# Attention with a row-wise maximum in the score matmul: the first 512 queries take their maxima by one more matmul, no early burst of maxima, and the weights lead both load queues

## The chip, the cores and the metric

The kernel runs on one core of one Trainium2 chip. The metric is the device time of one execution in microseconds (us). Three runs of the kernel before gave 602.68, 604.81 and 605.72 us; the median is 604.81 us.

Engines are called as the profile calls them: PE is TensorE's matmul, PEld its weight load, DVE is VectorE, ACT is ScalarE, POOL is GpSimd, SP is SyncE. SPq and ACTq are the sequencers of SP and ACT issuing transfers.

## The reference

One attention layer and one mixture-of-experts layer, each followed by a residual and a layer norm. The input is x of 2048 tokens by 128 channels, float32. Cut to what matters here:

```
k_eff = W_dq.T @ W_uq.T @ W_uk          # weights alone, folded per head
v_eff = W_uv.T @ W_o.T
c_kv  = x @ W_dkv.T
q_lat = (x @ W_dq.T @ W_uq.T) . k_eff    # 16 heads of 8 channels
attn  = softmax(causal(q_lat . c_kv / sqrt(8)))
y     = (attn . c_kv) . v_eff
x     = layernorm(x + y)
x     = layernorm(x + moe(x))            # 8 experts, top 2, capacity 80, two groups of 1024 tokens
```

The softmax of a row of scores needs that row's maximum, since the scores are large.

## The kernel before

**The parts ahead of attention.** SP issues the six weight transfers, ACT issues the four transfers of x (256 KB each) and the router's. PE first waits for all six weights (`s_w`), turns or multiplies them (L970 to L972), then turns the first block of x (`turn_x(0)`, L979), and alternates with DVE until the folded weights `qw`, `kw`, `vw` exist. From these it makes keys, queries (L999) and values (L1003) of each 512 tokens. Keys and queries are each split by ACT and DVE into three bf16 parts (L595 to L738), which SP stores to DRAM and loads again, laid out by head, into `kT` and `qT` (L437, L448), in transfers of 384 KB, or 96 KB for the first block's four head groups. Partitions 0 to 125 carry the products of parts; partitions 126 and 127 of `kT` hold ones, so that whatever stands in partitions 126 and 127 of `qT` is added to every score of that query.

**Attention.** The 2048 queries are four supers of 512; 16 heads are four groups of four. A unit is one super with one group of heads, so there are 16 units, units 0 to 3 being the first 512 queries. A unit of super s has 4(s+1) steps, one for each 128 keys, and 160 steps in all: `STEPS`, with `FIRST[u]` the first step of unit u (0, 4, 8, 12, 16, 24, ...). One step is, for each of four heads, one matmul `scT` of 128 keys by up to 512 queries (L1041), on a diagonal tile one more matmul of 128 columns that masks (L1045), an exponential on ACT (L629), and two steps later (`LAG`) the product with the values into `acc` (L1058, 8 matmuls). For the four steps of the first super the widths are 512, 384, 256 and 128 queries. `scT` is a ring of three banks (`SRING`).

**The maxima.** Before unit u can start, each of its rows needs its maximum. It is found from a second set of scores, `sc`, with the queries on partitions: for each item one matmul (L1020) of 128 to 512 columns and one DVE instruction (L749 for a full block, L754 for a diagonal one, which adds the mask) into `part_max`. `sc` is a ring of three banks too. Items of a unit of super 0 have 128, 256, 384 or 512 columns, four of each. `max_rows(u)` joins the partial maxima on DVE and splits the negative maximum in two bf16 halves, `turn_max(u)` turns them on PE (L1027) to 8 rows by 512 queries, `keep_maxT(u)` copies them on ACT to `maxT[u % 2]` (L610), and `max_to_rows(u)` issues a transfer from `maxT` into partitions 126 and 127 of `qT` (L615). PE waits for it before the unit's first score:

```python
if j == 0 and h == 0:
    pe.wait_ge(max_in[u % 2], 16 * (u // 2 + 1))
```

**The order.** Unit 0's 16 items are done ahead of the steps. Then `EARLY` = 16 items, those of unit 1, are issued in one burst before step 0, behind `turn_max(0)`. All further items are woven into the steps by `woven()`, between the four heads of a step. It fills from the last step backwards: an item of w columns counts w + 60, a step takes up to 2400, or `RUSH_WORK` = 3000 in the first `RUSH` = 20 steps, and no item of unit u may stand behind `max_step(u)` = `FIRST[u]` - `LEAD` - 1. `LEAD` is 5. `schedule()` puts `max_rows(u)` into step `max_step(u)` and the `max_turn` that calls `turn_max` and `keep_maxT` at the end of the step after it. Each engine runs its own program in this order; semaphores tie them.

**Behind the first super** (`FIRST[GROUPS]` on) come the normalisation and the experts, which run beside later attention steps. SP issues the experts' weights (2 MB each, L483 and L484) as soon as the splits are stored and loaded.

Of the kernel before, what the change touches and what calls it, by code (L numbers as in the profile page):

```python
# [26 lines left out]
P = 128  # L27
# [3 lines left out]
QUERIES = 512  # L31
SUPERS = T // QUERIES
TILES = T // P
QT = QUERIES // P
HG = 4
GROUPS = HEADS // HG
UNITS = SUPERS * GROUPS
# [6 lines left out]
PRING = 12  # L44
SRING = 3
AHEAD = 1
EARLY = 16
LEAD = 5
ITEM_WORK = 2400
RUSH, RUSH_WORK = 20, 3000  # L50
LAG = 2
BIG = -1e38

# [15 lines left out]
F32, BF16, U32 = mybir.dt.float32, mybir.dt.bfloat16, mybir.dt.uint32  # L69
ALU = mybir.AluOpType  # L70
# [5 lines left out]
def super_of(u):  # L76
    return u // GROUPS
# [7 lines left out]
FIRST = [sum(unit_steps(v) for v in range(u)) for u in range(UNITS + 1)]  # L85
# [8 lines left out]
def is_diagonal(u, j):  # L94
    return j >= QT * super_of(u)
# [11 lines left out]

def max_step(u):

    return max(0, FIRST[u] - LEAD - 1)  # L110


def item_work(i):
# [112 lines left out]
def program(nc, x_d, wdq_d, wuq_d, wdkv_d, wuk_d, wuv_d, wo_d, router_d, wi_d, wo2_d, out_d):  # L226
    ctx = ExitStack()
    with ctx:
        def sb(name, shape, dt=F32):
            return ctx.enter_context(nc.sbuf_tensor(name, shape, dt))  # L230

        def sem(name):
            return ctx.enter_context(nc.semaphore(name))
# [10 lines left out]
        x = sb("x", [P, TILES, C])  # L244
# [33 lines left out]
        wdq, wuq, wdkv, wuk = early(0, LAT, C), early(1, C, LAT), early(2, LAT, C), early(3, C, LAT)  # L278
        wuv, wo, wuqT, woT = early(4, C, LAT), early(5, C, C), early(6, LAT, C), early(7, C, C)
# [4 lines left out]
        ident16 = sb("ident16", [P, P], BF16)  # L284
# [11 lines left out]
        maxT = [sb(f"maxT{i}", [2 * HG, QUERIES], BF16) for i in range(2)]  # L296
# [26 lines left out]
        slot_out = sb("slot_out", [P, 2 * MT], U32)  # L323
        einT = sb("einT", [P, SLOTS])
        x1T = einT[:, 0:QUERIES]
        hT = [sb(f"hT{i}", [P, FC, CAP]) for i in range(2)]

        back2 = sb("back2", [P, MT, C])
# [2 lines left out]
        scT = [ctx.enter_context(nc.psum_tensor(f"scT{i}", [P, QUERIES], F32)) for i in range(SRING)]  # L331
# [5 lines left out]
        s_w = sem("s_w")  # L337
        s_router = sem("s_router")
        s_x = [sem(f"s_x{i}") for i in range(SUPERS)]
        s_ffw = sem("s_ffw")  # L340
        s_const = sem("s_const")
        s_const_v = sem("s_const_v")
        s_rows = sem("s_rows")
        q_rows = sem("q_rows")
        q_rows0 = sem("q_rows0")
# [17 lines left out]
        maxT_kept = sem("maxT_kept")  # L363
        max_in = [sem(f"max_in{i}") for i in range(2)]
        scT_made = sem("scT_made")
# [48 lines left out]
        def token_rows(d, a, b):  # L414
            return d[a * P:b * P, :].rearrange("(n p) c -> p n c", p=P)
# [2 lines left out]

        @block.sync
        def _(sp):  # L420
            for dst, src in ((wuq, wuq_d), (wuk, wuk_d), (wo, wo_d), (wdq, wdq_d), (wuv, wuv_d), (wdkv, wdkv_d)):
                sp.dma_start(dst, src).then_inc(s_w, 16)

            def clear_slots():
                sp.wait_ge(s_const, 3)
# [51 lines left out]
            for b in range(LAST + 1):  # L477
# [7 lines left out]
                for name, arg in TASKS[b]:  # L485
                    if name == "max_turn" and arg in (GROUPS + 1, 2 * GROUPS + 1):
                        s = super_of(arg) + 1
# [11 lines left out]
                    if name == "norm_out" and arg[0] == "moe":  # L499
                        k = arg[1]  # L500
# [6 lines left out]
        def _(pool):  # L507
# [12 lines left out]
            nc.gpsimd.affine_select(out=later16[:, :], in_=later16[:, :], compare_op=ALU.is_ge, fill=BIG, base=0,  # L520
                                    pattern=[[1, P]], channel_multiplier=-1).then_inc(s_const, 1)

            tri = causal[:, QUERIES - P:QUERIES]
            nc.gpsimd.affine_select(out=tri, in_=tri, compare_op=ALU.is_ge, fill=BIG, base=0,
                                    pattern=[[-1, P]], channel_multiplier=1).then_inc(s_const, 1)
# [42 lines left out]
            for b in range(LAST + 1):  # L568
                for name, arg in TASKS[b]:
                    if name == "slots" and arg < MOE_GROUPS - 1:  # L570
                        scatter(arg)
                    if name == "norm_ln" and arg[0] == "attn" and arg[1] < SUPERS - 1:
                        k = arg[1]
# [8 lines left out]

        @block.scalar
        def _(act):
            for i in range(SUPERS):
                act.dma_start(x[:, i * QT:(i + 1) * QT, :], token_rows(x_d, i * QT, (i + 1) * QT)).then_inc(s_x[i], 16)
            act.dma_start(router[:, :], router_d).then_inc(s_router, 16)
            nc.scalar.preload_act_table_set("natural_log_exp_and_others")
# [15 lines left out]

            def keep_maxT(u, bank):

                if u >= 2:

                    act.wait_ge(max_in[u % 2], 16 * (u // 2))
                nc.scalar.activation(maxT[u % 2][:, :], bank.bitcast(BF16)[0:2 * HG, 0:QUERIES], ACT.Copy).then_inc(maxT_kept, 1)  # L610

            def max_to_rows(u):
                act.wait_ge(maxT_kept, u + 1)
                g = u % GROUPS
                act.dma_start(qT[super_of(u) % 2][MROW:MROW + 2, g * HG:(g + 1) * HG, :], maxT[u % 2][:, :]).then_inc(max_in[u % 2], 16)  # L615
# [350 lines left out]
        def _(pe):  # L966
# [64 lines left out]
            def scores(b, h):  # L1031

                u, j = STEPS[b]
                s, off = super_of(u), first_query(u, j)
                if j == 0 and h == 0:
                    pe.wait_ge(max_in[u % 2], 16 * (u // 2 + 1))
                n = HG * b + h
                if n >= SRING:
                    pe.wait_ge(exp_done, n - SRING + 1)
                head = u % GROUPS * HG + h  # L1040
                ins = nc.tensor.matmul(scT[n % SRING][:, 0:QUERIES - off], kT[:, head, j * P:(j + 1) * P],  # L1041
                                       qT[s % 2][:, head, off:QUERIES], start=True, stop=True, skip_group_check=True)
                if is_diagonal(u, j):

                    ins = nc.tensor.matmul(scT[n % SRING][:, 0:P], ident16[:, :], later16[:, :], start=False, stop=True,  # L1045
                                           skip_group_check=True)
                ins.then_inc(scT_made, 1)
# [27 lines left out]
                scores_for_max(i)  # L1075
            pe.wait_ge(v_kept, SUPERS)
            pe.wait_ge(s_const_v, 2)
            pe.wait_ge(maxT_kept, AHEAD)

            def task(name, arg):  # L1080
# [107 lines left out]
```

## Time and profile before

| quantity | value |
|---|---|
| median of three runs | 604.81 us (602.68 to 605.72) |
| the profiled execution's own time | 605.5 us |
| its span | 603.8 us |
| mean granted TensorE clock | 0.958 |
| busy: PE, DVE, ACT, POOL | 87%, 74%, 58%, 10% |
| attention step 0 begins (first score matmul issued) | about 50.2 us |
| step 19 begins | about 110.8 us |

The span is from the first to the last instruction that the profile shows; the execution's time holds 1.7 us more. Busy shares are means over stages with different limits, so this text reads stretches of time. The time of a step's beginning is that of the first L1020 or L1041 matmul behind the step before it.

### The profile page before, as it was taken

The numbers are of one execution on the slowest core, as the hardware profiler recorded it, in microseconds if no ns is written. First come the engines' busy times: TensorE is split into PE (matmuls) and PEld (weight loads), VectorE is DVE, ScalarE is ACT, GpSimd is POOL, SyncE is SP. The second block draws the span as 40 slices with busy tenths as digits, with TensorE's granted clock in tenths as the row PEclk, the third lists the DMA queues.
The fourth block names the chain that finished last, engine by engine and source line by source line (L and its number), as shares of the span: only waits on it lengthen the run. The fifth ranks groups of instructions, "written<-read, shape, count | busy, mean of one in ns | idle before, by whom it ended". The sixth has DMA issues, their size and how long they took to land.

```text
span 603.8 us, 10349 instructions
## 1 busy us (share of the span) xinstructions
PE 523.9 (87%) x3445; PEld 220.7 (37%) x3491; DVE 447.2 (74%) x1311; ACT 349.5 (58%) x751; POOL 63.1 (10%) x64
## 2 busy tenths in 40 slices
PE   4966999889999989879989999899999988946990
PEld 2523333333333333234445333233333221223890
DVE  4786999798987988957657888879889814347616
ACT  0614556656767765755655777577777779820230
POOL 9400000000000000640000540000000000000040
PEclk9967999999999999999999999999999999985996
DMA  3489992200000300110000250000000000000024
GB/s 85 126 213 209 202 279 61 45 2 2 2 2 1 80 2 2 40 54 1 2 11 1 48 37 1 1 2 1 1 2 1 2 1 19 19 0 1 8 37 49
DMA packets 25410, 24.90 MB, mean 41 GB/s; under 512 B 2314, under 2 KB 22668, under 8 KB 25356
## 3 DMA queue, kind: packets, MB, share of 16 engines
q1 hardware_dynamic: 21660, 20.42, 13.9%
q0 software_dynamic: 1280, 2.62, 3.7%
q10 hardware_dynamic: 2416, 1.18, 0.7%
q8 instruction: 28, 0.46, 0.3%
q14 instruction: 26, 0.21, 0.1%
HBM read 16.81 MB, written 7.28 MB: 40 GB/s over the span
## 4 chain that ended last, share of the span: by engine, by line
PE 52%; issue 22%; DVE 13%; ACT 5%; DMA 3%; POOL 3%; ACTq 1%; SPq 0%; DVEq 0%; POOLq 0%
PE acc L1058 15%; PE sc L1020 13%; PE scT L1041 11%; DVE unused L754 3%; ACT probs L629 3%; POOL exp_in L551 2%; DVE part_max L749 2%; PE scT L1045 2%; PE ms L1143 2%; PE ms L1149 2%; DMA qT<-maxT 1%; DVE kT L909 1%; PE ms L1092 1%; ACT maxT L610 1%; DVE stats L783 1%
## 5 line engine op out<-in xcount | busy, mean ns | idle before, releaser
L629 ACT ACTIVATE probs<-scT 128x512 f32<-128x512 f32 (+3 forms) x640 | 302.6, 539 | 131.3 <-PE scT L1045 77.4
L749 DVE TENSOR_REDUCE part_max<-sc 128x1 f32<-128x512 f32 x384 | 249.9, 684 | 26.9 <-PE sc L1020 23.7
L1020 PE MATMUL sc<-kT,qT 126*128 126x512 bf16 (+3 forms) x640 | 223.2, 360 | 16.1 <-DVE part_max L749 7.6
L1041 PE MATMUL scT<-qT,kT 128*128 128x512 bf16 (+3 forms) x594 | 201.8, 349 | 10.1 <-ACT probs L629 8.6
L1058 PE MATMUL acc<-probs,v 128*9 128x512 f32 (+3 forms) x1280 | 146.5, 531 | 0.4
L754 DVE CUSTOM_DVE_ANT_0 unused<-sc,causal 128x128 bf16<-128x128 f32 (+3 forms) x256 | 120.2, 484 | 32.9 <-PE sc L1020 31.4
L1020 PEld LDWEIGHTS sc<-kT,qT 126*128 126x128 bf16 x640 | 62.4, 99 | 145.9 <-DVE part_max L749 82.9
L1041 PEld LDWEIGHTS scT<-qT,kT 128*128 128x128 bf16 x640 | 62.2, 99 | 70.6 <-ACT probs L629 39.9
L1045 PE MATMUL scT<-later,ident 128*128 128x128 bf16 x256 | 55.9, 221 | 4.9 <-DMA qT<-maxT 4.3
L1058 PEld LDWEIGHTS acc<-probs,v 128*9 128x9 f32 x1280 | 19.2, 88 | 47.3 <-ACT probs L629 33.2
L1045 PEld LDWEIGHTS scT<-later,ident 128*128 128x128 bf16 x256 | 25.6, 100 | 19.3 <-issue 0.7
L575 POOL TENSOR_TENSOR res<-res,x 128x512 f32<-128x512 f32 x3 | 3.8, 1269 | 227.3 <-DVEq L802 227.3
L810 DVE TENSOR_TENSOR nt<-rs 128x2 f32<-128x2 f32 (+1 forms) x12 | 1.9, 160 | 29.7 <-ACT rs L651 29.7
L754 DVE DVE_READ_ACCUMULATOR2_ANT part_max<- 128x1 f32 x256 | 21.2, 83 | 0.0
L565 POOL DMA_INDIRECT back<-exp_out,slot_out x16 | 15.3, 954 | 53.4 <-DMA exp_out<-x 48.9
L610 ACT ACTIVATE maxT<-ms 8x512 bf16<-8x512 bf16 x16 | 9.4, 586 | 16.1 <-PE ms L1027 16.1
L649 ACT ACTIVATE lnv<-var 128x4 f32<-128x4 f32 x12 | 2.6, 218 | 27.7 <-DVE var L938 27.7
L551 POOL DMA_INDIRECT exp_in<-x,slot_in x16 | 15.7, 980 | 24.8 <-DVE slot_in L877 20.2
L578 POOL IOTA kT<- 128x640 f32 x1 | 0.7, 665 | 147.6 <-PE scT L1045 147.6
L565 POOL DMA_INDIRECT x<-exp_out,slot_out x8 | 7.6, 956 | 72.9 <-DMA exp_out<-x 70.8
L794 DVE RECIPROCAL recip<-ms 128x16 f32<-128x16 f32 x13 | 3.3, 257 | 14.7 <-PE ms L1092 14.7
L531 POOL MEMSET kT<- 64x4096 uint32 x4 | 13.9, 3506 | 0.1
(182 smaller groups left out, 340.2 us busy)
## 6 DMA issues: line engine op xcount, KB each, us to landing
kT<-parts_k SPq DMA_DIRECT2D x9, 384.0 KB
qT<-parts_q SPq DMA_DIRECT2D x9, 384.0 KB
wi<-in_L_ffn_wi SPq DMA_DIRECT2D x1, 2048.0 KB, 18.1
parts_k<-wi SPq DMA_DIRECT2D x3, 384.0 KB, 4.1
parts_q<-wi SPq DMA_DIRECT2D x3, 384.0 KB, 5.0
kT<-parts_k SPq DMA_DIRECT2D x12, 96.0 KB
qT<-parts_q SPq DMA_DIRECT2D x12, 96.0 KB
x<-in_L_attn_x ACTq DMA_DIRECT2D x4, 256.0 KB, 4.3
```

What stands on the lines that cost most here:

```text
L531: nc.gpsimd.memset(rows, one_pair).then_inc(s_rows, 1)
L551: pool.indirect_dma_start(exp_in_d[:, :], bass.IndirectOffsetOnAxis(slot_in[:, n:n + 1], 0), x1[:, g * MT + n % MT, :], None).then_inc(sca ...
L565: pool.indirect_dma_start(dst, None, exp_out_d[g][:, :], bass.IndirectOffsetOnAxis(slot_out[:, n:n + 1], 0)).then_inc(gathered[PIECES * g ...
L610: nc.scalar.activation(maxT[u % 2][:, :], bank.bitcast(BF16)[0:2 * HG, 0:QUERIES], ACT.Copy).then_inc(maxT_kept, 1)
L629: nc.scalar.activation(probs[n % PRING][:, 0:width], scT[n % SRING][:, 0:width], ACT.Exp).then_inc(exp_done, 1)
L749: nc.vector.tensor_reduce(dst, sc[i % SRING][:, :], AX.X, ALU.max).then_inc(sc_used, 1)
L754: nc.vector.tensor_tensor_reduce(unused[i % 2][:, 0:w], sc[i % SRING][:, 0:w], causal[:, QUERIES - w:QUERIES], 1.0, 3 * BIG, ALU.add, ALU. ...
L1020: nc.tensor.matmul(sc[i % SRING][:, 0:w], qT[s % 2][0:MROW, head, qt * P:(qt + 1) * P], kT[0:MROW, head, c * QUERIES:c * QUERIES + w], sta ...
L1041: ins = nc.tensor.matmul(scT[n % SRING][:, 0:QUERIES - off], kT[:, head, j * P:(j + 1) * P], qT[s % 2][:, head, off:QUERIES], start=True, ...
L1045: ins = nc.tensor.matmul(scT[n % SRING][:, 0:P], ident16[:, :], later16[:, :], start=False, stop=True, skip_group_check=True)
L1058: ins = nc.tensor.matmul(acc[32 * h:32 * h + VC, off:QUERIES], v[:, j, head, :], probs[(HG * b + h) % PRING][:, 0:QUERIES - off], start=(j ...
L1143: ins = nc.tensor.matmul(bank[:, f * CAP:(f + 1) * CAP], wi[:, e, f * P:(f + 1) * P], einT[:, e * CAP:(e + 1) * CAP], start=True, stop=True)
```

## The change

It does six things. (1) For units 0 to 3 the maxima no longer go by a transfer to `qT`: after each score matmul a second one adds them into the same bank, with `maxT` (8 rows by the step's queries) as the moving side and a constant `pick16` as the stationary side, which picks rows h and h + 4 for head h; PE waits for ACT's copy instead of the transfer. From unit 4 on nothing changes there. (2) `EARLY` becomes 0: unit 1's items are woven into steps 0 and 1. (3) `LEAD` becomes `LEADS`: 2 for units 0 to 3, 3 for unit 4, 5 for the others. (4) `RUSH_WORK` becomes 3300. (5) The weights are issued three on SP and three on ACT, and behind them x blocks 0 and 2 on SP, 1 and 3 on ACT. (6) POOL makes `pick16` with one more instruction, before it fills the rows of ones.

```diff
-EARLY = 16
-LEAD = 5
+EARLY = 0
+LEADS = [2] * GROUPS + [3] + [5] * (UNITS - GROUPS - 1)
 ITEM_WORK = 2400
-RUSH, RUSH_WORK = 20, 3000
+RUSH, RUSH_WORK = 20, 3300
...
-    return max(0, FIRST[u] - LEAD - 1)
+    return max(0, FIRST[u] - LEADS[u] - 1)
+
+
+def rows_sent(u):
+
+    return max(0, len(range(u % 2, u + 1, 2)) - len(range(u % 2, GROUPS, 2)))
...
+        pick16 = einT[0:2 * HG, 0:HG * P // 2].bitcast(BF16).rearrange("p (h k) -> p h k", h=HG)
...
         def _(sp):
-            for dst, src in ((wuq, wuq_d), (wuk, wuk_d), (wo, wo_d), (wdq, wdq_d), (wuv, wuv_d), (wdkv, wdkv_d)):
+            for dst, src in ((wuq, wuq_d), (wdq, wdq_d), (wdkv, wdkv_d)):
                 sp.dma_start(dst, src).then_inc(s_w, 16)
+            for i in range(0, SUPERS, 2):
+                sp.dma_start(x[:, i * QT:(i + 1) * QT, :], token_rows(x_d, i * QT, (i + 1) * QT)).then_inc(s_x[i], 16)
...
+            nc.gpsimd.tensor_tensor(pick16[:, :, :], ident16[0:2 * HG, 0:HG].unsqueeze(2).to_broadcast([2 * HG, HG, P]),
+                                    ident16[0:2 * HG, HG:2 * HG].unsqueeze(2).to_broadcast([2 * HG, HG, P]), ALU.add).then_inc(picked, 1)
...
         def _(act):
-            for i in range(SUPERS):
+            for dst, src in ((wo, wo_d), (wuk, wuk_d), (wuv, wuv_d)):
+                act.dma_start(dst, src).then_inc(s_w, 16)
+            for i in range(1, SUPERS, 2):
                 act.dma_start(x[:, i * QT:(i + 1) * QT, :], token_rows(x_d, i * QT, (i + 1) * QT)).then_inc(s_x[i], 16)
...
             def keep_maxT(u, bank):
-                if u >= 2:
-
-                    act.wait_ge(max_in[u % 2], 16 * (u // 2))
+                if 2 <= u < GROUPS + 2:
+
+                    act.wait_ge(scT_made, HG * FIRST[u - 1])
+                elif u >= 2:
+
+                    act.wait_ge(max_in[u % 2], 16 * rows_sent(u - 2))
...
             def max_to_rows(u):
+                if super_of(u) == 0:
+                    return
...
                 if j == 0 and h == 0:
-                    pe.wait_ge(max_in[u % 2], 16 * (u // 2 + 1))
+                    if s:
+                        pe.wait_ge(max_in[u % 2], 16 * rows_sent(u))
+                    else:
+                        pe.wait_ge(maxT_kept, u + 1)
...
+                if s == 0:
+
+                    nc.tensor.matmul(scT[n % SRING][:, 0:QUERIES - off], pick16[:, h, :], maxT[u % 2][:, off:QUERIES],
+                                     start=False, stop=True, skip_group_check=True)
...
             pe.wait_ge(s_const_v, 2)
+            pe.wait_ge(picked, 1)
```

Worked out from the two versions of `woven()`, the items of each stretch of steps are these; from step 19 on both orders are the same:

| steps | items, columns before | items, columns after |
|---|---|---|
| ahead of step 0 (unit 1) | 16, 5120 | 0 |
| 0 to 3 | 24, 6656 | 26, 7424 (10, 6, 0, 10 in the four steps) |
| 4 to 7 | 25, 9728 | 30, 10496 |
| 8 to 11 | 22, 9600 | 24, 10752 |
| 12 to 15 | 22, 9344 | 27, 10752 |
| 16 to 18 | 18, 6912 | 20, 7936 |

## Rows read from the trace of the kernel before

**Rows 1.** The page: busy shares, and the span in 40 equal slices.

```profile
PE 523.9 (87%) x3445; PEld 220.7 (37%) x3491; DVE 447.2 (74%) x1311; ACT 349.5 (58%) x751; POOL 63.1 (10%) x64
...
PE   4966999889999989879989999899999988946990
```

**Rows 2.** The chain that ended last, in order of time: start us, us, what.

```profile
3.45 4.26 DMA wo<-in_L_attn_W_dkv
...
40.49 0.60 ACT maxT L610
41.10 9.00 DMA qT<-maxT
```

**Rows 3.** Windows: us, busy (instructions) of each engine, granted clock, DMA share, GB/s.

```profile
40.70:47.50 6.80, 5.42 (x15) 1.34 (x13) 6.77 (x32) 0.38 (x1) 0.00 (x0) 0.50 0.83 147
47.50:50.60 3.10, 0.00 (x0) 0.14 (x2) 0.03 (x2) 0.00 (x0) 0.00 (x0) 0.50 0.84 157
50.60:63.00 12.40, 11.45 (x80) 5.77 (x80) 9.95 (x54) 7.08 (x17) 0.00 (x0) 0.85 0.98 255
63.00:76.50 13.50, 12.26 (x94) 5.01 (x95) 12.51 (x44) 7.53 (x18) 0.00 (x0) 1.00 0.92 182
76.50:89.50 13.00, 11.88 (x90) 4.85 (x90) 12.17 (x37) 7.44 (x18) 0.00 (x0) 1.00 1.04 290
89.50:101.70 12.20, 11.63 (x88) 4.67 (x88) 11.26 (x33) 7.49 (x18) 0.00 (x0) 1.00 0.16 52
101.70:112.00 10.30, 9.91 (x59) 3.01 (x61) 10.04 (x33) 7.67 (x15) 0.00 (x0) 1.00 0.59 118
```

**Rows 4.** Timeline of the first 21 us: start, us, engine, line, what, idle before.

```profile
0.81 2.14 ACTq L586 DMA_DIRECT2D x<-in_L_attn_x  x4
...
2.30 3.47 DVE L705 MEMSET qT<- 64x4096 uint32 x1 [0.91 <-issue]
...
7.84 0.39 PE L970 MATMUL sc<-ident,wo 128*64 128x128 f32 x1 [7.84 <-DMA wo<-in_L_attn_W_dkv]
...
8.78 1.12 PE L979 MATMUL scT<-ident,x 128*128 128x128 f32 x4
...
20.39 0.60 PE L979 MATMUL scT<-ident,x 128*128 128x128 f32 x4
```

**Rows 5.** DMA issues of the first weights and of x, us to landing.

```profile
wo<-in_L_attn_W_uq SPq DMA_DIRECT2D x1, 32.0 KB, 2.4
...
DMA to landing us min/median/max: 3.3/4.3/4.9
```

**Rows 6.** Timeline of PE in unit 3: scores, masks, and the value products.

```profile
90.18 0.38 PE L1041 MATMUL scT<-qT,kT 128*128 128x512 bf16 x1
90.40 0.22 PE L1045 MATMUL scT<-later,ident 128*128 128x128 bf16 x1
...
97.67 1.05 PE L1058 MATMUL acc<-probs,v 128*9 128x512 f32 x8
...
98.87 0.22 PE L1041 MATMUL scT<-qT,kT 128*128 128x128 bf16 x1
98.93 0.22 PE L1045 MATMUL scT<-later,ident 128*128 128x128 bf16 x1
```

**Rows 7.** Timeline of DVE in items of 128 and of 512 columns.

```profile
40.71 0.29 DVE L754 CUSTOM_DVE_ANT_0 unused<-sc,causal 128x128 bf16<-128x128 f32 x1 [0.99 <-PE sc L1020]
40.92 0.08 DVE L754 DVE_READ_ACCUMULATOR2_ANT part_max<- 128x1 f32 x1
40.92 0.29 DVE L754 CUSTOM_DVE_ANT_0 unused<-sc,causal 128x128 bf16<-128x128 f32 x1
...
100.89 0.68 DVE L754 CUSTOM_DVE_ANT_0 unused<-sc,causal 128x512 bf16<-128x512 f32 x1
101.50 0.08 DVE L754 DVE_READ_ACCUMULATOR2_ANT part_max<- 128x1 f32 x1
```

**Rows 8.** Timeline of ACT: unit 4's copy and its transfer.

```profile
89.61 0.59 ACT L610 ACTIVATE maxT<-ms 8x512 bf16<-8x512 bf16 x1 [0.69 <-PE ms L1027]
90.23 0.64 ACTq L615 DMA_DIRECT2D qT<-maxT  x1
```

**Rows 9.** Windows around the end of the bulk transfers.

```profile
92.00:94.00 2.00, 2.00 (x20) 0.93 (x18) 1.88 (x6) 1.89 (x5) 0.00 (x0) 1.00 0.14 41
```

**Rows 10.** POOL's nearest elementwise instruction: duration min, median, max in ns.

```profile
L575 POOL TENSOR_TENSOR res<-res,x x3: 1262/1267/1277, 127.5 to 382.2; 128x512 f32<-128x512 f32 x3
```

More of the change, by code:

```diff
@@ L342, in program @@
         s_const_v = sem("s_const_v")
+        picked = sem("picked")
         s_rows = sem("s_rows")
```

## The prediction, made before the changed kernel ran

> **What bounds the kernel now.** I read the page first: PE is busy 87% of the span and DVE 74%, and the first slices show PE at 4, 9, 6 and 6 tenths [rows 1]. These are means; the change touches only the stretch up to step 18, because both orders are the same from step 19 on. So I read that stretch alone. The chain of waits shows two transfers that end last there. One is a weight, issued at 3.45 us and landing 4.26 us later. The other is unit 0's row of maxima, 9.00 us from 41.10 to 50.10 [rows 2]. The windows then say what was done in those 9 us: the early burst keeps DVE busy 6.77 us, then DVE has 0.03 us of work in 3.10 us, and PE none [rows 3]. From 50.6 us on, DVE is busy 9.95 of 12.4, then 12.51 of 13.5, 12.17 of 13.0, 11.26 of 12.2 and 10.04 of 10.3 us [rows 3]. PE's busy shares are as high, but they count each matmul's tail: a 128-column matmul counts 0.22 us while the next starts 0.06 us after it [rows 6]. By starts, a 512-column matmul takes 0.22 us and a 128-column one 0.055 us. DVE, not PE, sets the pace of the woven steps: an item costs it 0.21 us at 128 columns and 0.61 us at 512 [rows 7], that is 0.08 us plus 0.133 per 128 columns, while PE needs 0.055 per 128.
>
> I measure the stretch from ACT's copy of unit 0's maxima (ready at 41.1 us) to the start of step 19 (110.8 us): 69.7 us.
>
> **The load end, edits 5 and 6.** PE's first instruction waits 7.84 us for the last weight; x is there before it, since the first turning of x at 8.78 follows with no wait [rows 4]. ACT issues all four x transfers from 0.81 to 2.95 us, so SP's late weights run beside 1 MB of x. Afterwards each queue issues three weights at about 0.5 us each, the last at about 1.9 us. The first weight took 2.4 us to land and an x block at least 3.3 us [rows 5]. So the weights are there at about 4.4 and x block 0, issued at about 2.4, at about 5.8 us. PE's three weight products (0.94 us, 7.84 to 8.78) are done by then, and DVE's memset of `qT` ends at 5.77 [rows 4], just in time. The first turning starts at 5.8 instead of 8.78: 3.0 us earlier. With the median 4.3 us to landing and an issue as late as 2.8, it is 7.1 and 1.7 us. The same shift should pass down the chain of PE and DVE to 41.1 us, as each link is released by the one before it. One thing may not shift: the turning of four x tiles counts 1.12 us at 8.78 and 0.60 at 20.39 [rows 4], though the granted clock reads 1.00 in both places, so PE speeds up somewhere before 20.4 us. If that moment stays fixed in time, about half of a microsecond per microsecond of shift is lost. I take 2.6 us, bounds 1.2 and 3.3. POOL's extra instruction on 8 partitions is bounded by 0 and the 1.27 us of a 128x512 one [rows 10]. It delays the first memset of ones, which ended near 7 us and is first needed by a load at 24.6 us; I take nothing. If that cover went, it would cost its 1.27 us.
>
> **The row transfer and the burst, edits 1 and 2.** The 9.0 us wait of unit 0 goes. What it covered does not: the burst's 16 items cost DVE 16 x 0.08 + 40 x 0.133 = 6.6 us (6.77 in the window [rows 3]) and are now woven in. Only DVE's idle time can be won: the 3.1 us ahead of step 0 plus about 0.4 us until the first new item, and whatever later idle goes.
>
> The Trainium skill, page "DMA: Bandwidth & Descriptors", section "Anatomy of one DMA — SWDGE (gpsimd) path", gives a transfer a fixed 2.0 us. The trace does not agree for this one: 9.0 us for 8 KB, at a DMA share of 0.83 [rows 2, 3]. By the page's figure the burst would already hide the wait, nothing would be won at step 0, and the sum below would be about 603.5; the measured 9.0 us is what I use.
>
> **The picks, edit 1.** Sixteen steps of four heads get one matmul more: 64 of them, 4 x 4 x (512 + 384 + 256 + 128) = 20480 columns. No row shows a matmul with an 8-row moving side. The nearest is the mask matmul, accumulating into the same bank straight behind the score matmul with no gap [rows 6]. At 0.055 us per 128 columns the picks take PE 8.8 us, 2.2 us a unit. The lower bound is nothing on the path, where PE waits for DVE anyway; the upper is all 8.8 us. The weight loads run beside the matmuls as the others do.
>
> **The new order, edits 2 to 4.** After the change a unit of steps 4 to 15 costs PE: scores and picks 10240 columns 4.4, masks 0.9, values about 2.6 (0.97 for a 512-wide step by starts, less for the narrower) [rows 6], items about 4.6, turning 0.2: 12.7 us. DVE has 10496, 10752 and 10752 columns: 13.3, 13.1 and 13.3 us, plus about 0.5 us of `max_rows`, so 13.8, 13.6, 13.8. DVE still leads over a unit, but in each unit's widest step PE needs about 3.6 us against DVE's 3.4, so taking the larger in each step gives 14.1, 13.8 and 14.1. Steps 16 to 18 are 9.85 + 0.5, so 10.4. Steps 0 to 3 have 7424 columns, 9.8 + 0.5 on DVE; but step 0 has 4608 score, pick and mask columns and 2304 item columns, and the granted clock is at 0.5 (1.2 GHz) when it starts. After the restart at 50.6 us it averaged 0.85 over 12.4 us [rows 3], which is 3.7 us at half; the same here makes 4440 columns in 3.7 us and the other 2472 in 1.0, so 4.7 us on PE against 3.2 on DVE, and step 2 has no items, which leaves DVE about 0.9 us idle. I take 13.0. The sum is 13.0 + 14.1 + 13.8 + 14.1 + 10.4 = 65.4 us. The same sum for steps 4 to 18 before is 12.6 + 12.2 + 12.0 + 9.1 = 45.9 against 47.8 measured (63.0 to 110.8), 1.9 us of small waits through the three-bank rings. With PE at some 90% instead of 75% these grow: I take 2.5 us. That makes 67.9 us against 69.7: a gain of 1.8 us.
>
> The bounds: the stretch's DVE work is 62.7 us (sum of the seven windows' DVE time [rows 3]); with 0.4 us to start, 63.1 is the floor, a gain of 6.6. If the picks lie wholly on the path, the stretch is 69.7 − 9.4 (start of step 0) + 6.8 (burst items) + 8.8 = 75.9, a loss of 6.2, which the work sums make unlikely; half on the path is 71.5, a loss of 1.8.
>
> The shorter leads cost nothing for units 1 to 3: PE reaches the turning one step, some 3 us, after DVE's last item, and ACT's copy takes 0.6 us [rows 8] within the following step. ACT's copy of unit 2 waits for the scores of unit 0, long done. For unit 4 the transfer stays. Its turning ends step 13; 1.5 us later it is issued, and two steps (about 6.5 us) after the turning PE wants it: 5.0 us to land. It is issued at about 89 us, when the bulk is ending (before, the share is 0.14 by 92 [rows 9], and the load end moves it earlier). I cost it at nothing; bounds 0 and 4.0, if it takes 9.0 us as unit 0's did.
>
> **The sum.** 2.6 + 1.8 = 4.4 us. The profiled execution took 605.5 us (span 603.8 and 1.7 around it) and would take 601.1. It stood 0.7 above the median of 604.81, so the prediction is 600.4 us.
>
> **The rivals.**
> - *The picks hide wholly behind DVE.* For it: DVE leads every unit's sum. Against: PE would have almost no slack in the wide steps. The stretch is near its floor: 6.6 + 2.6 = 9.2 us, 595.6.
> - *PE becomes the bound (the slower side).* The place is steps 0 to 15, the price 8.8 us of picks. It decides once more than about 60% of them lie on the path: the 2.6 us of the load end and 9.4 − 6.8 = 2.6 of the wait are then used up. At 90% the time is 604.8 − 2.6 − 2.6 + 7.9 = 607.5. For it: PE's busy share already reads above 0.9 [rows 3], and ring waits make a coupled pair slower than either. Against: the spacing by starts.
> - *The load end gives nothing*, because the same 1.2 MB still lands by about 7.5 us: 604.8 − 1.8 = 603.0. The Trainium skill speaks for this one: "DMA: Bandwidth & Descriptors", section "Issuing engines are not separate DMA queues", says that issuing from two engines saves only sequencer time. No row shows what the weights would do ahead of x.
> - *Unit 4's row comes late* by up to 4.0 us at step 16, in place of unit 0's: 604.4.
>
> **How the numbers follow.** Forecast 0.46, spread 598.5 to 602.5; picks hidden 0.14; PE the bound 0.15; load end empty 0.14; unit 4 late 0.11. Three us, 0.5%, is about what a measurement can tell from no change. Faster by more than that: most of the forecast (0.42) and the hidden picks (0.14), 0.56. Same: the empty load end, unit 4 late, the forecast's rest, 0.31. Slower: 0.13. The range of 596 to 605 leaves out most of the PE-bound case and the end of the hidden one.
>
> **What would show it.** Right: the first turning of x near 5.8 us, unit 0's copy on ACT ready near 38.5, the first score matmul within 0.5 us of it, step 19 at about 106.4; DVE busy 61 to 63 us in between with 5 to 6 us idle; no PE wait on a transfer at step 16. Wrong: a first turning after 7.5 us; DVE waiting for PE's `sc` by more than 8 us; a PE wait on `qT<-maxT` near 100 us; or a granted clock of 0.5 that outlasts step 0.

## The result, and the profile after

The changed kernel took 617.74 us (median of four runs, 616.52 to 618.49) against 604.75 for the kernel before: a ratio of 1.022, 95% interval 1.020 to 1.024. It is 13.0 us slower. 600.4 us with a range of 596 to 605 was forecast. Two runs, both of front_only below (609.6 and 1724.5 us), were disturbed and count in no ratio.

The page of the changed kernel, busy shares and the new group, the pick matmul, which is L1068 here (the columns are busy time, mean ns, idle time before):

```profile
PE 544.2 (88%) x3509; PEld 224.8 (36%) x3555; DVE 449.5 (73%) x1311; ACT 351.6 (57%) x751; POOL 64.1 (10%) x65
...
L1068 PE MATMUL scT<-maxT,einT 8*128 8x512 bf16 (+3 forms) x64 | 21.6, 337 | 0.8 <-issue 0.4
```

PE is busy 20.3 us more than before, DVE 2.3 [rows 1]. The added PE time is not the 8.8 us of columns that the prediction counted.

Timeline of the changed kernel's first 8 us and of ACT's copy of unit 0's maxima:

```profile
4.73 0.39 PE L990 MATMUL sc<-ident,wo 128*64 128x128 f32 x1 [4.73 <-DMA wo<-in_L_attn_W_dkv]
...
6.85 1.12 PE L999 MATMUL scT<-ident,x 128*128 128x128 f32 x4 [1.10 <-DMA x<-in_L_attn_x]
...
18.64 0.95 PE L999 MATMUL scT<-ident,x 128*128 128x128 f32 x4
...
39.10 0.59 ACT L628 ACTIVATE maxT<-ms 8x512 bf16<-8x512 bf16 x1 [9.15 <-PE ms L1047]
```

The weights lead: PE begins 3.1 us earlier than in [rows 4], waits 1.1 us for x, and turns it 1.9 us earlier. The copy comes 1.4 us earlier [rows 2]. So the load end works, by 1.4 us. Everything after it is worse. Windows of the changed kernel, cut at about the first score of units 1, 2, 3 and 4; the first begins just ahead of ACT's copy:

```profile
38.50:62.60 24.10, 22.75 (x97) 7.49 (x98) 11.30 (x55) 8.16 (x18) 0.00 (x0) 0.55 0.89 219
62.60:79.60 17.00, 16.71 (x117) 6.17 (x114) 14.42 (x59) 8.06 (x18) 0.00 (x0) 1.00 1.00 207
79.60:96.20 16.60, 16.45 (x112) 5.99 (x110) 14.02 (x39) 8.06 (x18) 0.00 (x0) 1.00 0.51 161
96.20:113.20 17.00, 16.52 (x111) 6.06 (x111) 14.04 (x43) 7.85 (x18) 0.00 (x0) 1.00 0.01 2
```

DVE is busy for 14.0 to 14.4 of some 17 us a unit, where it had 12.51 of 13.5 [rows 3]: it waits for PE, and PE is the bound. The view of waits in 38 to 124 us (engine, line, what it waited for: us in total, times, longest) says so too:

```profile
DVE unused L774 <- PE sc L1040: 17.6, 22, 4.9
```

The first window has a second trouble. Its mean granted clock is 0.55, though PE is busy 22.75 of 24.10 us. Finer windows of the changed kernel show when it rose:

```profile
56.00:60.00 4.00, 4.00 (x25) 1.62 (x25) 1.20 (x9) 1.25 (x3) 0.00 (x0) 0.50 0.94 319
60.00:62.00 2.00, 1.99 (x16) 0.95 (x18) 1.80 (x11) 0.59 (x3) 0.00 (x0) 0.93 0.84 236
```

PE ran at 0.5, that is 1.2 GHz, until just after 60 us, through some 20 us in which it was busy all the time. The spacing inside a head shows the other part. PE and its weight loads (PEld) in unit 2 of the changed kernel, at full clock:

```profile
80.92 0.38 PE L1064 MATMUL scT<-qT,kT 128*128 128x512 bf16 x1
81.23 0.38 PE L1068 MATMUL scT<-maxT,einT 8*128 8x512 bf16 x1
81.55 0.23 PE L1072 MATMUL scT<-later,ident 128*128 128x128 bf16 x1
81.61 0.49 PE L1040 MATMUL sc<-kT,qT 126*128 126x256 bf16 x2
...
81.23 0.09 PEld L1068 LDWEIGHTS scT<-maxT,einT 8*128 8x128 bf16 x1 [0.43 <-issue]
81.54 0.10 PEld L1072 LDWEIGHTS scT<-later,ident 128*128 128x128 bf16 x1 [0.23 <-issue]
```

A 512-column score is followed by the next matmul after 0.22 us in [rows 6], and here after 0.31. The pick is followed by the mask after 0.32. The pick's weight load does not start until the score's columns are through (81.23), nor the mask's load until the pick's are (81.54). Each change, from 128 rows to 8 and back, shows a load of 0.09 to 0.10 us. That is 0.2 us a pick on top of its 0.22 us of columns.

### The profile page after: what moved, and what is told of

Read it like the earlier page. It is cut to its first block, busy times and chain, and to the rows that moved or that the text cites. A ratio compares the mean times of both kernels' runs of the same rounds, so it can differ in the third digit from the quotient of the medians.

```text
span 616.5 us, 10474 instructions
## 1 busy us (share of the span) xinstructions
PE 544.2 (88%) x3509; PEld 224.8 (36%) x3555; DVE 449.5 (73%) x1311; ACT 351.6 (57%) x751; POOL 64.1 (10%) x65
## 4 chain that ended last, share of the span: by engine, by line
PE 57%; issue 20%; DVE 11%; ACT 5%; POOL 3%; DMA 2%; ACTq 1%; SPq 0%; DVEq 0%; POOLq 0%
PE acc L1085 15%; PE sc L1040 14%; PE scT L1064 12%; PE scT L1072 3%; PE scT L1068 3%; ACT probs L649 2%; POOL exp_in L564 2%; DVE unused L774 2%; DVE part_max L769 2%; PE ms L1171 1%; PE ms L1177 1%; DVE kT L929 1%; ACTq L635 1%; PE ms L1120 1%; ACT maxT L628 1%
## 5 line engine op out<-in xcount | busy, mean ns | idle before, releaser
L1040 PE MATMUL sc<-kT,qT 126*128 126x512 bf16 (+3 forms) x640 | 219.8, 359 | 14.4 <-DVE part_max L769 6.4
L774 DVE CUSTOM_DVE_ANT_0 unused<-sc,causal 128x128 bf16<-128x128 f32 (+3 forms) x256 | 121.2, 485 | 42.2 <-PE sc L1040 40.5
L1068 PE MATMUL scT<-maxT,einT 8*128 8x512 bf16 (+3 forms) x64 | 21.6, 337 | 0.8 <-issue 0.4
L578 POOL DMA_INDIRECT back<-exp_out,slot_out x16 | 15.2, 953 | 53.5 <-DMA exp_out<-x 48.9
L628 ACT ACTIVATE maxT<-ms 8x512 bf16<-8x512 bf16 x16 | 9.4, 586 | 17.6 <-PE ms L1047 17.5
```

What stands on the lines that cost most here:

```text
L578: pool.indirect_dma_start(dst, None, exp_out_d[g][:, :], bass.IndirectOffsetOnAxis(slot_out[:, n:n + 1], 0)).then_inc(gathered[PIECES * g ...
L774: nc.vector.tensor_tensor_reduce(unused[i % 2][:, 0:w], sc[i % SRING][:, 0:w], causal[:, QUERIES - w:QUERIES], 1.0, 3 * BIG, ALU.add, ALU. ...
L1040: nc.tensor.matmul(sc[i % SRING][:, 0:w], qT[s % 2][0:MROW, head, qt * P:(qt + 1) * P], kT[0:MROW, head, c * QUERIES:c * QUERIES + w], sta ...
L1068: nc.tensor.matmul(scT[n % SRING][:, 0:QUERIES - off], pick16[:, h, :], maxT[u % 2][:, off:QUERIES], start=False, stop=True, skip_group_ch ...
```

## The experiments

Line numbers differ a little between the kernels; the tiles' names tell which matmul is meant. All times stand against runs of the kernel before on the same chip.

### The picks on 128 rows, the order alone, the picks alone, the loads alone

**pad128** keeps all six edits, but widens the pick with rows of zeros:

```diff
-        maxT = [sb(f"maxT{i}", [2 * HG, QUERIES], BF16) for i in range(2)]
+        maxT = [sb(f"maxT{i}", [P, QUERIES], BF16) for i in range(2)]
-        pick16 = einT[0:2 * HG, 0:HG * P // 2]...
+        pick16 = einT[:, 0:HG * P // 2]...
```

(and a memset of `maxT` on POOL). Expected:

> The changed kernel, but with maxT and pick16 on all 128 partitions (rows 8 to 127 zero), so that the pick is a 128-row matmul with the same columns. Theory A (the switch): an 8-row matmul between 128-row ones keeps its own weight load and the next one's from running beside a matmul, about 0.1 us each, so 64 picks cost some 13 us beyond their columns; here the spacing from score to pick and from pick to mask falls from 0.31 and 0.32 us to about 0.22 and 0.22 at 512 columns, and the time from 617.7 to about 604 us. Theory B (the order): the time was lost by the missing burst and the shorter leads, whatever the picks' shape; the spacing may fall, but the time stays above 614 us. Theory C (the columns alone): the picks cost by their columns, and nothing changes by more than 1 us.

Measured: 603.98 us against 604.63, ratio 0.999 (0.998 to 1.000), 13.8 us under the changed kernel. Timeline of PE in its unit 3:

```profile
83.32 0.38 PE L1069 MATMUL scT<-qT,kT 128*128 128x512 bf16 x1
83.54 0.38 PE L1073 MATMUL scT<-maxT,einT 128*128 128x512 bf16 x1
83.76 0.22 PE L1077 MATMUL scT<-later,ident 128*128 128x128 bf16 x1
83.81 0.38 PE L1045 MATMUL sc<-kT,qT 126*128 126x512 bf16 x1
```

0.22, 0.22 and 0.05 us: the same columns with no load showing. The pick's load now starts 0.01 us after the score instead of behind it (PEld of pad128):

```profile
83.33 0.10 PEld L1073 LDWEIGHTS scT<-maxT,einT 128*128 128x128 bf16 x1
83.54 0.10 PEld L1077 LDWEIGHTS scT<-later,ident 128*128 128x128 bf16 x1
```

And the clock rose in the first step instead of after 20 us (windows of pad128):

```profile
40.00:42.00 2.00, 1.89 (x9) 1.10 (x10) 0.93 (x7) 0.53 (x1) 0.00 (x0) 0.50 0.84 150
42.00:44.00 2.00, 2.00 (x11) 1.01 (x10) 1.39 (x9) 0.94 (x3) 0.00 (x0) 0.74 0.87 123
```

Theory A's number is met, in part by luck: it put all 13 us down to the loads and had no term for the clock, to which some 5 of them belong (pad64 below). Theories B and C fall as explanations of the 13 us.

**order_only** is the kernel before with `EARLY = 0`, `LEADS` and `RUSH_WORK = 3300`. Expected:

> The kernel before with edits 2 to 4 alone (no burst, the shorter leads, 3300 per step); the rows still go by transfer, the loads as before. Theory A: the order costs little of the 13 us; step 0 still waits for the 9 us transfer, now with nothing under it, and unit 1's row may be late as well, so 604.8 plus 3 to 9 us: 608 to 614, and no part of it is PE's own work. Theory B: PE and DVE are out of step through units 0 to 3 even beside those waits, DVE idle on PE over 15 us in steps 0 to 15: 615 or more.

Measured: 615.70 us, ratio 1.019 (1.016 to 1.023). That is above theory A's 608 to 614 and at the lower edge of theory B's number, and DVE's 17.5 us of waiting for PE are over the 15 that theory B asked for. But half of them lie under a row transfer, so they are not waits beside it. The view of waits in 36 to 110 us, the two that matter:

```profile
DVE unused L754 <- PE sc L1020: 17.5, 11, 8.7
PEld scT L1041 <- DMA qT<-maxT: 13.2, 3, 8.5
```

Three times PE waits for a row transfer, the longest 8.5 us at step 0. DVE's longest wait for PE, 8.7 us, is under that one. So the new order is costly where rows still go by transfer: it needs the picks. This run does not tell what it costs beside them, and which share of the other 8.8 us of DVE's waiting belongs to the two later transfers stays open.

**picks_only** is the changed kernel with edits 2 to 5 undone. Expected:

> The changed kernel with edits 2 to 5 undone: burst of 16 items, lead 5, 3000 per step, loads as before; only the 8-row picks in place of the row transfers of units 0 to 3, and POOL's constant. Theory A: the picks alone cost more than the whole change did, since the load end's gain is missing: 64 x 0.4 = 26 us of PE time, less what DVE's pace hides (about 3 us a unit) and less the 3 us wait that goes: 604.8 + 10 to 16, so 615 to 621. Theory B: 604.8 + 8.8 of columns at most, less 3: under 610.

Measured: 619.76 us, ratio 1.025 (1.023 to 1.027), inside theory A's range. The picks alone, with the burst and the old leads, lose more than the whole change. Four of its five runs took 619.4 to 621.0 at a mean granted clock of 0.950; the profiled one took 612.9 at 0.959. In its trace the clock had risen to 1.00 by about the first pick (45.93 us), and stayed there (windows of picks_only):

```profile
44.00:48.00 4.00, 4.00 (x16) 1.15 (x15) 3.20 (x14) 1.22 (x3) 0.00 (x0) 0.80 0.85 140
48.00:52.00 4.00, 4.00 (x24) 1.60 (x23) 3.41 (x20) 2.64 (x5) 0.00 (x0) 1.00 0.94 191
```

So 8-row picks did not bring a risen clock down. Mean clocks of 0.950 and 0.959 over some 615 us are, by estimate, about 12 us more at 0.5, and the same program then took about 7 us more: the nearest thing here to a price of the clock by itself.

**front_only** is the kernel before with edit 5 alone. Expected:

> The kernel before with edit 5 alone: weights three on each queue, x behind them on both. All theories: the first turning of x at 6.85 us as in the changed kernel, unit 0's copy on ACT 1.4 us earlier, and the time 604.8 - 1.4 = 603.4 us (602.5 to 604). If unit 0's row transfer, which ends the wait at step 0, is bound by the bulk transfers around it and not by when it is issued, it is 604.5 or more.

Measured: 603.23 us, ratio 0.996 (0.994 to 0.998). The median is the 1.4 us that were expected. The interval allows 1 to 4 us, and the profiled run, which took 599.23 us, does not show the expected steps (timeline of ACT in front_only):

```profile
37.93 0.59 ACT L614 ACTIVATE maxT<-ms 8x512 bf16<-8x512 bf16 x1 [9.14 <-PE ms L1031]
45.24 3.44 ACT L633 ACTIVATE probs<-scT 128x512 f32<-128x512 f32 x6 [6.72 <-PE scT L1049]
```

Its copy stands 2.6 us earlier than before, not 1.4, and its row transfer took 5.83 us from 38.55, not 9.00. So the load end gives something, but this run does not pin it to 1.4 us, and the 9.0 us of the wait are no constant either: in order_only the three transfers that PE waited for took 8.77, 4.16 and 6.50 us.

### How many rows it takes

**double8** puts a second 8-row matmul with zero weights behind each pick:

```diff
+                    nc.tensor.matmul(scT[n % SRING][:, 0:QUERIES - off], zero8[:, :], maxT[u % 2][:, off:QUERIES],
+                                     start=False, stop=True, skip_group_check=True)
```

> The changed kernel with a second 8-row matmul behind each pick, of the same width, with zero weights (it adds nothing to the scores). Theory A (the load is exposed at each change between 8 and 128 rows): from pick to second pick the spacing is that of the columns, 0.22 us at 512, and 8.8 us in all are added, at most: 617.7 + 6 to 9 = 624 to 627. Theory A2 (every matmul of few rows pays some 0.1 us by itself, whatever stands ahead of it): the spacing from pick to second pick is 0.31 us, and 15 us are added: 630 to 633.

Measured: 628.34 us, 10.6 above the changed kernel. Timeline of PE, at 128 columns:

```profile
82.82 0.22 PE L1066 MATMUL scT<-qT,kT 128*128 128x128 bf16 x1
82.97 0.23 PE L1070 MATMUL scT<-maxT,einT 8*128 8x128 bf16 x1
83.04 0.21 PE L1072 MATMUL scT<-maxT,zero 8*128 8x128 bf16 x1
83.19 0.23 PE L1076 MATMUL scT<-later,ident 128*128 128x128 bf16 x1
```

From 8 rows to 8 rows it takes 0.07 us; into 8 rows 0.15 and out of them 0.15. It is the change that costs, not the small matmul. Theory A2 wanted 0.15 in the middle and 630 us or more. The total is somewhat above theory A's 624 to 627, which counted every added column at full clock; here the granted clock still reads 0.50 in the window from 60 to 64 us. Of the 11.0 us between the two profiled runs, 1.2 lie ahead of ACT's copy (40.32 against 39.10 us), where the kernels do the same work, and 9.8 between the copy and step 19.

**pad64** and **pad96** are pad128 with 64 and 96 partitions.

> As pad128, but with maxT and pick16 on 64 partitions. Theory A in its strict form (only a matmul whose rows reach the whole array lets the next load run beside it): spacings 0.31 and 0.32 us at 512 columns as with 8 rows, and 614 to 618 us. Its loose form (few rows are the trouble, half the array is enough): spacings 0.22 us and 604 us as pad128. The granted clock tells a second thing: with 8 rows it stayed at 0.5 until 60 us, with 128 it rose at 43 us. If it follows the rows it rises in between; if it follows how closely the matmuls stand, it goes with the spacings.

> As pad128, with maxT and pick16 on 96 partitions: the last test of the row count. If a matmul has to reach into the last quarter of the rows for the next load to run beside it (the 126-row matmuls of the maxima do, and hide their loads), the spacings stay at 0.31 and 0.32 us at 512 columns and the time at 609 to 614 us, as with 64 rows. If 96 rows are already enough, the spacings are 0.22 us and the time is 604 us.

Measured: pad64 613.17 us, ratio 1.016 (1.013 to 1.019); pad96 604.29, ratio 1.001 (0.999 to 1.004). PE in pad64, from a score to the maxima's matmul behind the mask, then in pad96, from a score to the mask:

```profile
57.62 0.38 PE L1069 MATMUL scT<-qT,kT 128*128 128x512 bf16 x1
57.93 0.39 PE L1073 MATMUL scT<-maxT,einT 64*128 64x512 bf16 x1
58.25 0.23 PE L1077 MATMUL scT<-later,ident 128*128 128x128 bf16 x1
58.32 0.38 PE L1045 MATMUL sc<-kT,qT 126*128 126x512 bf16 x1
```

```profile
79.87 0.22 PE L1069 MATMUL scT<-qT,kT 128*128 128x128 bf16 x1
79.93 0.22 PE L1073 MATMUL scT<-maxT,einT 96*128 96x128 bf16 x1
79.99 0.22 PE L1077 MATMUL scT<-later,ident 128*128 128x128 bf16 x1
```

With 64 rows the spacings are those of 8 rows (0.31, 0.32), as the strict form said, though the time is 0.8 us under its 614 to 618; with 96 they are those of 128 (0.06 at 128 columns). The guess that a matmul has to reach into the last quarter of the rows falls: 96 are enough, 64 are not. What lies between was not tried, and why 64 and 96 rows differ is not shown.

pad64 also splits the 13.8 us between changed kernel and pad128. Its spacings are the changed kernel's, but its clock rose earlier (windows of pad64):

```profile
42.00:44.00 2.00, 2.00 (x8) 0.61 (x8) 0.78 (x4) 0.60 (x1) 0.00 (x0) 0.50 0.85 116
44.00:46.00 2.00, 2.00 (x9) 0.69 (x8) 1.39 (x6) 0.69 (x2) 0.00 (x0) 0.70 0.83 156
```

By the medians, 617.7 − 613.2 = 4.5 us go with a clock that rose 15 us later, and 613.2 − 604.0 = 9.2 us with the loads that show. By the three traces, from the end of ACT's copy to the first exponential of step 19, it is 84.5 − 78.9 = 5.6 and 78.9 − 70.0 = 8.9 us. The 64 picks add 64 x 0.2 = 12.8 us of PE time, of which the rest lay beside waits. The split is good to some two us, because pad64's four runs spread over 7 us: 610.4, 612.9, 613.4 and 617.4 us at mean granted clocks of 0.966, 0.961, 0.961 and 0.953. The last is the changed kernel's time at the changed kernel's clock (617.7 at 0.948 to 0.953).

So the clock is not settled by the rows alone. In the traces of these three kernels it rose after 60 us with 8 rows, by 46 with 64 and by 44 with 128. But one run in four with 64 rows has the mean clock and the time of the 8-row kernel, and one in five of picks_only, with 8 rows, had its clock up at the first pick. In these runs a late rise is more frequent with few rows; why is not shown.

### What is left of the change when the picks are priced right

**pad_old_order** is pad128 with burst, leads and limit as before; **unit0_pick** has 128-row picks for unit 0 alone beside the old order and the new loads.

```diff
-EARLY = 0
-LEADS = [2] * GROUPS + [3] + [5] * (UNITS - GROUPS - 1)
+EARLY = 16
+LEAD = 5
-RUSH, RUSH_WORK = 20, 3300
+RUSH, RUSH_WORK = 20, 3000
+PICKED = 1
...
-                if s == 0:
+                if u < PICKED:
                     nc.tensor.matmul(scT[n % SRING][:, 0:QUERIES - off], pick16[:, h, :], ...
```

(`PICKED` and its test are unit0_pick's only.)

> 128-row picks for units 0 to 3 and the new loads, but burst, lead and limit as before (16, 5, 3000). If the new order loses time that the padded picks won (DVE idle in step 2 and at the start of step 0), this is faster than pad128: step 0 starts behind the burst at about 45 us, 604.6 - 1.4 (loads) - 3.5 (wait) + 1 to 3 (picks) = 601 to 603. If the burst is as costly as the wait it covers, it is 604 as pad128.

> 128-row picks for unit 0 alone, units 1 to 3 by transfer as before, the new loads, burst, lead and limit as before. Only 16 picks of 2.2 us of columns in all, where PE has slack. 604.6 - 1.4 - 3.5 + 0 to 1 = 599.7 to 600.7. If step 0 cannot use the earlier start because DVE sets the pace up to step 18, it is the 3.1 us of DVE idle that is won and no more: 600.1. If the gain of the start is given back behind it, 603 or more.

Measured: pad_old_order 600.74 us, just under its 601 to 603, ratio 0.994 (0.992 to 0.995); unit0_pick 599.94, as expected, ratio 0.992 (0.990 to 0.994), the lowest median of all. Windows of unit0_pick from the first item of the burst to step 0, and from there to 63 us:

```profile
39.70:45.10 5.40, 5.24 (x13) 1.60 (x15) 5.38 (x27) 0.05 (x1) 0.00 (x0) 0.50 0.84 139
45.10:63.00 17.90, 16.56 (x125) 8.27 (x126) 15.12 (x73) 10.21 (x24) 0.00 (x0) 0.96 0.93 208
```

DVE is busy all of the first window; the 3.10 us in which it had 0.03 us of work [rows 3] are gone, since step 0 follows the burst at once. The load end (1.4) and this stall (3.1) make 4.5 of unit0_pick's 5.2 us; the other 0.7 is within the spread of its runs (598.96 to 600.93). Its trace against that of the kernel before has the same places: the copy is 1.3 us earlier, from the end of the copy to the first exponential it takes 6.3 us instead of 9.9, and steps 0 to 18 take 60.5 us as before's 60.4.

**units01_pick** has 128-row picks for units 0 and 1 and no burst (`LEADS = [2, 2, 3] + [5] * 13`, 3300); **units01_half** half a burst (`EARLY = 8`, `LEADS = [2, 2, 4] + [5] * 13`, 3100).

> 128-row picks for units 0 and 1, units 2 and 3 by transfer, no burst, leads 2, 2, 3 and then 5, 3300 per step, the new loads. If what costs the new order its time is unit 1's maxima in a PE-bound step 0 (the burst costs DVE 6.6 us but no PE time, step 0 without it is held by PE), this is 603 to 604 us, as pad128. If it is the idle stretches of DVE behind the short leads (none in step 2 here, one in step 11), it is at or under unit0_pick's 599.9 us.

> As units01_pick, with half the burst (8 items) and 3100 per step: step 0 starts some 2.5 us after the copy of unit 0's maxima. The two readings are as for units01_pick: between 599 and 601 if a short burst covers the way to ACT and back and no more, 602 or more if items in steps 0 and 1 cost more there than in the burst.

Measured: 603.30 us, ratio 0.999 (0.997 to 1.001), and 600.13, ratio 0.993 (0.991 to 0.995). With no burst, whether all four units are picked (pad128) or two, 603 to 604 us; with half or all of it, 600 to 601. DVE's busy time in the same 12.3 us of pad128 and of unit0_pick (windows, in this order):

```profile
39.70:52.00 12.30, 11.72 (x81) 6.29 (x81) 9.16 (x48) 6.75 (x17) 0.00 (x0) 0.86 0.88 156
```

```profile
39.70:52.00 12.30, 11.97 (x59) 5.42 (x61) 11.13 (x58) 4.60 (x10) 0.00 (x0) 0.72 0.87 149
```

The burst gives DVE 2.0 us more work in this stretch, beside PE's way to ACT and back and while PE's clock is still at 0.5. But this alone does not account for the times. The same window of units01_pick (603.30 us) and of units01_half (600.13 us), in this order:

```profile
39.70:52.00 12.30, 10.94 (x69) 5.82 (x71) 10.28 (x54) 5.87 (x13) 0.00 (x0) 0.87 0.90 167
39.70:52.00 12.30, 11.51 (x57) 5.40 (x58) 9.73 (x48) 5.49 (x11) 0.00 (x0) 0.77 0.90 168
```

The faster of the two has less DVE work there. The traces agree better over the whole stretch, from the end of the copy to the first exponential of step 19 (us):

| kernel | its profiled run | stretch | DVE busy | DVE idle | of it ahead of step 0's first exponential |
|---|---|---|---|---|---|
| before | 605.5 | 70.3 | 61.7 | 8.6 | 3.5 |
| units01_pick | 604.9 | 71.1 | 61.7 | 9.4 | 1.2 |
| pad128 | 603.7 | 70.0 | 62.3 | 7.7 | 1.2 |
| units01_half | 600.1 | 68.5 | 61.6 | 7.0 | 0.4 |
| pad_old_order | 599.5 | 68.3 | 62.1 | 6.2 | 0.0 |
| unit0_pick | 600.5 | 66.8 | 61.6 | 5.2 | 0.0 |

(The old loads put the copy of the kernel before 1.3 to 2.3 us later than the others'.) DVE's work is the same to 0.8 us in all six, so what a version wins is DVE idle time that it removes. The burst removes 1.2 us of it at the start. The rest lies in gaps inside the steps, and which difference of the orders makes those is not shown: units01_half also differs in its leads and limit.

## Why the prediction was wrong, step by step

**The load end: right in kind, too large.** 2.6 us were taken, 1.4 measured, inside the bounds of 1.2 to 3.3. x landed at 6.85 us, not 5.8, and of the 1.9 us won there 0.5 were lost on the way. That is the case that the prediction named, half of it: turning four tiles counts 0.95 us at 18.64, between the slow 1.12 and the fast 0.60, so PE speeds up at about 19.4 us. Before, its last eight turnings ahead of 20.39 count 1.68, between 1.91 and 1.05:

```profile
18.86 1.68 PE L1003 MATMUL scT<-wo 128*128 128x128 f32 x8
```

That puts the speed-up at about 20.3 (both are estimates from these durations). It moved by 0.9 us where x moved by 1.9, and half of the missing 1.0 is the 0.5 that was lost. This moment differs between runs: in pad96 the eight turnings at 16.80 already take 1.05 us, and its copy is at 38.05. So 1.4 us is what this pair of traces shows; over the ten traces with the new loads the copy stands at 37.9 to 40.3 us (median 38.9), against 39.9 to 40.5 in the three with the old. The Trainium skill, page "DMA: Bandwidth & Descriptors", section "Issuing engines are not separate DMA queues", spoke for the rival in which this end gives nothing. front_only decides against that: its interval leaves out nothing gained (0.994 to 0.998), though its trace does not confirm the 1.4 us step by step.

**The picks: the failed step.** "At 0.055 us per 128 columns the picks take PE 8.8 us" and "The weight loads run beside the matmuls as the others do." The nearest row, the mask matmul, has 128 rows like its neighbours, and the pick has 8. That difference was named ("No row shows a matmul with an 8-row moving side") and then priced at nothing, also in the upper bound. What the runs showed in its place is 0.31 + 0.32 − 0.22 = 0.41 us for a 512-column pick against 0.22: 12.8 us more over 64 picks, of which about 9 reach the end (9.2 by medians, 8.9 by traces). The Trainium skill, page "TensorE: Matmul & The Clock Gate", section "LDWEIGHTS (loading the stationary operand)", says that a load's time goes by its columns and not its rows. The trace agrees: 0.09 us with 8 rows, 0.10 with 128. It is whether the load runs beside a matmul that went by the rows.

**The clock: the second failed step.** "The same here makes 4440 columns in 3.7 us and the other 2472 in 1.0" took the clock to rise as after the restart in [rows 3]. In the traces it took some 20 us with 8-row picks, about 6 with 64 rows and about 3 with 128. The forecast's own list of what would make it wrong had this ("a granted clock of 0.5 that outlasts step 0"), and also DVE waiting for PE's `sc` by more than 8 us (17.6 here). The clock's cost is about 5 us: 4.5 by the medians, 5.6 by the traces, with pad64's spread on both.

**The sum of the new order: right in the steps, short at their ends.** The first exponentials of steps 0, 4, 8, 12, 16 and 19 are the marks:

| stretch of steps | forecast | pad128 | changed kernel |
|---|---|---|---|
| 0 to 3 | 13.0 | 13.0 | 22.1 |
| 4 to 7 | 14.1 | 15.2 | 17.1 |
| 8 to 11 | 13.8 | 14.3 | 16.5 |
| 12 to 15 | 14.1 | 15.4 | 16.5 |
| 16 to 18 | 10.4 | 10.4 | 10.4 |
| sum | 65.4, with waits 67.9 | 68.3 | 82.5 |

With the picks at the price that was assumed (pad128) the sum holds to 0.4 us, small waits included. What it left out are the 1.7 us from the copy to the first exponential: the stretch began at the copy, and step 0 without a burst has two items, a score, a pick and a mask ahead of it at half clock. With that, the stretch takes 70.0 us as before's 70.3, and the order's gain is nothing. The load end short by 1.2 us and the stretch short by 1.5 are 2.7 of the 3.6 us between 600.4 and pad128's 604.0; the rest is about the spread of the runs. The hidden wait of 9 us, on which edits 1 and 2 rest, was real, but 6.6 us of it were DVE work that had to be done anyway, and without the burst DVE's idle time only moved: 8.6 us in this stretch before, 7.7 in pad128. (The bounds took 9.4 us for the start of step 0. From 41.1 to 50.2 it is 9.1, which changes neither bound by more than 0.3.)

**The rivals.** "PE becomes the bound" was the one that came, at the place named (steps 0 to 15), forecast at 607.5 with a chance of 0.15. Its price was set at 8.8 us of picks. pad128 has these same columns and stands at 604.0, so they are not what it cost: about 9 us are the loads that show and about 5 the clock, 13.8 together. "Unit 4's row comes late" did not come: the changed kernel has no PE wait on `qT<-maxT`. "The picks hide wholly" did not either, even with 128 rows. The figure of 2.0 us that the prediction set against the 9.0 comes from a section on transfers that GpSimd issues, and this one is issued by ACT; it bore on no term of the sum.

## What to carry to other kernels

A small-K matmul between full ones is not priced by its columns. If its rows differ enough from its neighbours' (8 or 64 against 128 here), the weight loads on both sides of it show. Pad it with zero rows, which cost nothing in columns (96 were enough here): 13.8 us in this kernel, with what the clock gave back. Before removing a wait, subtract the work that has been placed under it. Here 9.0 us of wait were 3 us of idle time, and the version that took just those (one unit's picks, burst kept) beat the kernel before by 5 us and the changed one by 18.

## What the runs showed of the hardware that was not expected

- Weight loads show at a change of rows: 8 to 128 and back 0.15 us each way at 128 columns against 0.06, the same at 64 rows (0.31 against 0.22 at 512 columns), none at 96. Between two 8-row matmuls 0.07 us.
- The granted clock stayed at 0.5 through some 20 us in which PE's busy time filled its windows, with 8-row picks; with 128-row picks in the same order it had risen within about 3 us. It is not the rows alone: one of four runs with 64 rows had the 8-row kernel's mean clock (0.953), and a clock that was up before the first 8-row pick stayed up (picks_only).
- An 8 KB row transfer beside the bulk took 9.00 us in one trace and 5.83 in another, at DMA shares of 0.83 and 0.82 (before; front_only).
- The Trainium skill's page "TensorE: Matmul & The Clock Gate", section "Back-to-back issue gap", gives a 128-column pair of load and matmul about 81 ns in a real kernel. The trace does not agree: 0.055 to 0.06 us here ([rows 6], pad96).
- Six weights ahead of x on two queues landed 3.1 us earlier than beside it, and x's first block still only at 6.85 us (in the other traces with the new loads the weights were there at 4.2 to 5.7 us and x at 6.7 to 8.0).
